# A four-layer sequence model in one launch: layer seams reworked, and the softmax layer's modulation moved from ScalarE to VectorE with one Silu per row of blocks

## The chip, the cores and the metric

The program runs on one core of one Trainium2 chip. The metric is the device time of one execution in microseconds (us), less being better. A change of under 0.2% either way can't be told from no change.

## The reference

The input x is 8 batches of 512 tokens by 512 channels, all float32. It passes four layers in order, each of which adds to x.

```python
# layers 0 and 1 (linear attention), 16 and 8 heads, masks on k and v
xn = layernorm(x); q, k, v = xn @ Wq + bq, xn @ Wk + bk, xn @ Wv + bv
q = softmax(q, over the head's channels); k = softmax(k, over tokens)
y = q @ (k.T @ v)                        # per head
# layer 2 (softmax attention), 16 heads of 32 channels
y = softmax(q @ k.T + mask) @ v
# the end of layers 0 to 2
scale, shift = split(silu(cond) @ W_emb + b_emb)
h = layernorm(y) * (1 + scale) + shift
x = x + silu(h) @ W_out + b_out
# layer 3 (two selective scans, forward and backward)
s = layernorm(x) * (1 + scale) + shift; u = layernorm(s)
z = (u @ Wz + bz) @ Wc + bc; y = scan(z) + z * D      # twice
x = x + gate * ((silu(u @ Wx + bx) * (y1 + y2)) @ Wf + bf + s)
```

## The kernel before

The program is a chain of six blocks, each with its own instruction streams for SP (SyncE, which issues nearly all transfers), TensorE, VectorE (DVE), ScalarE (ACT) and GpSimd (POOL). They run one after the other: `prologue` (folded weights, and the modulation tables `gain` and `shift`), `attention_layer` for layers 0 and 1, `softmax_layer` for layer 2, `front_layer` (norms and input products of layer 3) and `scan_layer`. The place between two blocks is called a seam here. At a seam the block's semaphores are cleared and all engines meet in a barrier (`sems.clear()`, L100). Activations go from layer to layer through HBM tensors `x1`, `x2`, `x3`, one batch (1 MB) at a time. Batch 0 of the next layer is read back, normed and put in `ahead["xn"]` before the seam, and the next K and Q weights are loaded before it too.

**Attention layers.** SP loads the column constants `cols`, the mask row `mask_in`, `rows`, `block_mask` and `keep_in`, then weights 2 and 3, then batch 1. Its last act in a layer is to wait until both `out` buffers are stored (L699). TensorE turns `xn` (stage T, drained by ScalarE with `cols` as scale and bias, L747), then projects K and Q; VectorE drains these, K with `mask_add` and Q with `rows`. Ahead of that VectorE waits for `cols_loaded` and for `const_loaded` (L887, L888), computes `keep`, tells the others that the PSUM banks are free (`absent`, L1018), and computes the mask (L908 or L911). GpSimd meanwhile adds a bias row to all of batch 0 (`residual`, L722).

**Softmax layer.** A batch is 16 steps of four heads and 128 queries. In each step TensorE makes four score tiles (L1303), turns the four tiles of exponentials of the step (L1314) and multiplies the turned tiles of the step before with V (L1330). VectorE takes scores and maxima out of PSUM (L1469) and copies two of the four turned tiles (L1478). ScalarE does four Exp (L1219) and copies the other two (L1228). Work around the attention of batch b is spread over these steps by a list written at build time, `slots`: 28 parts per batch, four each of YT(b-1), T(b+1), K(b+1), TY(b-1), Q(b+1), O(b-1), V(b+1), at most two per step, and all through the one PSUM bank `f_bank`. So each part on TensorE waits until the part before it has been taken out (`filler`, L1256), by the engine that `ENGINE` (L1035) names. TY is the turned, normed y: four transposes, and ScalarE then does Silu with the modulation as scale and bias (L1210). Its four parts stand in steps 7, 7, 8 and 9 of a batch, the first part of Q also in step 9, and the first part of O in step 11. The last batch has YT, TY and O of itself after the last step.

**Front layer.** Per batch TensorE turns `xn`, makes the dlt, B and C columns (L1735, L1743) and mx (L1753, L1700 is its Silu). VectorE does the norms of batch b+1 meanwhile, which end in `xn` (L1820); GpSimd raises the variances to the power of -0.5 (`rsqrt`, L1653) and makes `resid` in three passes over 1 MB (L1663, L1666, L1669). Its order is rsqrt(b), rsqrt2(b), residual(b), and residual(b) starts when `xs` of batch b is there. Batch 0's columns are turned last (`c_turn(B - 1)`), after which C is stored.

**Scan layer.** ScalarE issues loads of `wdt`, `neg_a`, `ident`, `half` and then negates the exponential of `neg_a`; SP loads the first set of `dlt` and `b_tm`, the first `w_z`, then `xn_t`. Every engine waits for all four constants (`const_loaded`). In the steady part GpSimd multiplies states by C (L2034) and VectorE scans (L2350).

The lines with these waits, quoted:

```python
                for j in range(2):
                    sp.wait_ge(x_stored[j], B // 2 * 16 + 16)        # L698, attention layers
    ENGINE = {"YT": "dve", "T": "act", "K": "act", "TY": "act", "Q": "act", "O": "dve", "V": "dve"}   # L1035
                    pool.wait_ge(xs_ready, (b + 1) * TT)             # L1657, residual(b) of the front layer
```

## Time and profile before

| | us |
|---|---|
| median of 3 runs | 5771.74 (5764.97 to 5774.0) |
| profiled execution, its time | 5768.94 |
| its span, first to last instruction | 5766.9 |
| prologue, to about | 200.8 |
| layer 0, to about | 820 |
| layer 1, to about | 1424 |
| layer 2, to about | 2655 |
| front layer, to about | 2992 |
| scan layer, to the end | 5767 |

Busy over the whole span are TensorE 94%, VectorE 73%, ScalarE 52%, GpSimd 50%; the mean granted TensorE clock is 0.984 of full speed. The profile numbers time from the first instruction. In a row of the timeline the last bracket tells how long the engine had been idle before the instruction and which instruction or transfer ended that idle time. A busy share over the span says little here, because the six blocks have different limits; the stretches around the seams and one batch of the softmax layer have to be read each for itself.

### The profile page before, as it was taken

Reading aid. Unit: us, or ns where it says so; the run is one execution under the profiler, and the core shown is the slowest. Engines: PE = TensorE matmul, PEld = TensorE weight load, DVE = VectorE, ACT = ScalarE, POOL = GpSimd, SP = SyncE. Lnnn points to the kernel's source line nnn. Section 1 sums busy time; section 2 is a strip of 40 time slices with the busy share of each in tenths; the row PEclk is TensorE's granted clock in tenths of the full one; section 3 lists DMA queues with packets and bytes.
Section 4 is the critical chain, followed back from the end, with each engine's and each line's share of the span. In section 5 each row is a group of like instructions: output and inputs, shape, how many; then the busy total and the mean of one; then the engine's idle time right before and its main releaser. Section 6 shows DMA issues by size and latency. Waiting matters only on the chain. (4 is left out here: it accounts for less than half of the span.)

```text
span 5766.9 us, 136480 instructions
## 1 busy us (share of the span) xinstructions
PE 5425.2 (94%) x58478; PEld 3270.1 (57%) x58478; DVE 4202.6 (73%) x5872; ACT 2982.9 (52%) x5007; POOL 2907.2 (50%) x956
## 2 busy tenths in 40 slices
PE   8899989998898888987989999999999999999998
PEld 3555545554455555543445566666666666666665
DVE  1455545554455555574429999999999999999996
ACT  0122212222455555551227677777777777776774
POOL 0000000000000000003329999999999999999997
PEclk9999989999999999998999999999999999999999
DMA  6200020111000000003440111212021121111211
GB/s 233 73 33 33 31 70 18 34 34 62 18 1 18 18 18 18 18 19 124 176 152 14 60 57 62 69 54 71 23 62 65 61 70 53 59 35 61 66 59 32
DMA packets 146443, 321.98 MB, mean 56 GB/s; under 512 B 27705, under 2 KB 28474, under 8 KB 135626
## 3 DMA queue, kind: packets, MB, share of 16 engines
q1 hardware_dynamic: 142994, 308.71, 15.8%
q8 instruction: 447, 7.32, 0.5%
q10 hardware_dynamic: 2880, 4.95, 0.2%
q14 instruction: 122, 1.00, 0.1%
HBM read 238.72 MB, written 74.89 MB: 54 GB/s over the span
## 5 line engine op out<-in xcount | busy, mean ns | idle before, releaser
L2034 POOL TENSOR_TENSOR sc_state<-sc_state,sc_c_rows 128x2048 f32<-128x2048 f32 x512 | 2331.3, 4568 | 123.9 <-DVE sc_state L2350 122.7
L2350 DVE TENSOR_TENSOR_SCAN sc_state<-sc_decay,wide 128x512 f32<-128x512 f32 x2048 | 2335.4, 1199 | 27.9 <-PE wide L2208 20.8
L2208 PEld LDWEIGHTS wide<-sc_diag,sc_du_t 64*64 64x64 f32 x32768 | 1047.8, 133 | 526.8 <-issue 344.4
L2208 PE MATMUL wide<-sc_diag,sc_du_t 64*64 64x128 f32 x32768 | 1218.7, 272 | 19.9 <-DVE sc_state L2350 19.7
L2224 PE MATMUL wide<-sc_state,sc_half 64*64 64x512 f32 x8192 | 1199.0, 591 | 7.4 <-POOL sc_state L2034 7.0
L2142 ACT ACTIVATE sc_decay<-sc_delta,sc_neg_a 128x512 f32<-128x512 f32 x1024 | 723.6, 719 | 448.6 <-DVE sc_state L2350 443.5
L2142 ACT ACTIVATE sc_decay<-sc_delta_x,sc_neg_a 128x512 f32<-128x512 f32 x1024 | 710.1, 717 | 286.7 <-DVE sc_state L2350 282.5
L1469 DVE CUSTOM_DVE_ANT_0 l_prob<-wide,l_mask_add 128x512 f32<-128x512 f32 x512 | 339.9, 683 | 275.8 <-PE wide L1303 275.8
L2224 PEld LDWEIGHTS wide<-sc_state,sc_half 64*64 64x64 f32 x8192 | 405.6, 133 | 168.2 <-issue 126.8
L1219 ACT ACTIVATE l_prob<-l_prob,l_s_max 128x512 f32<-128x512 f32 x512 | 366.0, 716 | 231.3 <-DVE l_s_max L1469 231.0
L2181 PE MATMUL wide<-sc_xn_t,sc_w_z 128*128 128x512 f32 x1024 | 476.8, 608 | 1.3 <-DMA sc_xn_t<-xn_d 1.3
L713 POOL TENSOR_SCALAR l_rstd<-l_mv 128x4 f32<-128x4 f32 x16 | 3.8, 236 | 713.9 <-DVE l_mv L902 713.9
L1314 PE MATMUL wide<-ahead_ident,l_prob 128*128 128x128 f32 x2048 | 292.0, 280 | 68.5 <-DVE l_prob_t L1478 41.0
L1314 PEld LDWEIGHTS wide<-ahead_ident,l_prob 128*128 128x128 f32 x2048 | 225.2, 142 | 225.5 <-issue 134.5
L1173 POOL TENSOR_TENSOR l_out<-ahead_x_wk,l_rows 128x2048 f32<-128x2048 f32 x8 | 36.3, 4537 | 603.6 <-DMA x<-l_out 592.0
L2181 PEld LDWEIGHTS wide<-sc_xn_t,sc_w_z 128*128 128x128 f32 x1024 | 185.2, 191 | 210.6 <-issue 210.6
L529 PE MATMUL wide<-l_xn_t,ahead_x_wk 128*128 128x512 f32 x512 | 228.3, 604 | 24.6 <-ACT l_xn_t L747 22.8
L2236 PE MATMUL wide<-sc_w_out,sc_y_sum 128*128 128x256 f32 x1024 | 244.4, 383 | 6.6 <-DVE sc_o_gated L2337 3.6
L747 ACT ACTIVATE l_k_tm<-wide 128x512 f32<-128x512 f32 x64 | 33.1, 606 | 379.4 <-PE wide L520 379.4
L538 PE MATMUL wide<-ahead_w,l_h_t 128*128 128x512 f32 x512 | 226.1, 600 | 1.7 <-ACT l_h_t L747 1.7
L538 PE MATMUL wide<-ahead_w,l_xn_t 128*128 128x512 f32 x512 | 222.5, 592 | 1.0 <-PEq L84 1.0
L538 PE MATMUL wide<-ahead_xn_wq,l_xn_t 128*128 128x512 f32 x512 | 222.5, 592 | 0.6 <-PEq L84 0.6
(240 smaller groups left out, 6983.3 us busy)
## 6 DMA issues: line engine op xcount, KB each, us to landing
sc_c_rows<-c_d SPq DMA_DIRECT2D x64, 1024.0 KB, 4.9
sc_w_z<-wz_tiles SPq DMA_DIRECT2D x128, 256.0 KB, 2.8
x<-l_out SPq DMA_DIRECT2D x24, 1024.0 KB, 4.8
ahead_x_wk<-x SPq DMA_DIRECT2D x16, 1024.0 KB, 6.3
mx_d<-fr_mx SPq DMA_DIRECT2D x16, 1024.0 KB, 4.5
sc_mx<-mx_d SPq DMA_DIRECT2D x64, 256.0 KB, 2.8
pro_wc<-in_wcT SPq DMA_DIRECT2D x4, 2048.0 KB, 19.2
xn_d<-fr_xn_t SPq DMA_DIRECT2D x8, 1024.0 KB, 4.1
```

The source lines that it names most:

```text
L529: last = pe.matmul(bank_of(name, m)[:, :], weight[:, k, m * P:(m + 1) * P], xn_t[:, k, :], start=(k == 0), stop=(k == DT - 1))
L538: last = pe.matmul(bank_of(name, t)[:, :], src_t[:, k, t * P:(t + 1) * P], weight[:, k, :], start=(k == 0), stop=(k == DT - 1))
L1219: act.activation(prob[:, u % (2 * HG), :], prob[:, u % (2 * HG), :], ACT.Exp, scale=-1.0, bias=s_max[:, u % (2 * HG):u % (2 * HG) + 1], ac ...
L1314: last = pe.transpose(t_banks[u % 2][:, m * P:(m + 1) * P], prob[:, u % (2 * HG), m * P:(m + 1) * P], ident[:, :])
L1469: dve.tensor_tensor_reduce(out=prob[:, u % (2 * HG), :], in0=s_banks[i], in1=mask_add[b % 2][:, :], op0=ALU.add, op1=ALU.min, scale=-1.0, ...
L2034: pool.tensor_tensor(state[quad % STATES][:, :, :], state[quad % STATES][:, :, :], c_rows[(r * 4 + q) % ROWS][:, :, :], ALU.mult).then_inc ...
L2142: act.activation(decay[step % DECAYS][:, :], of[:, :], ACT.Exp, scale=neg_a[:, s, m, n:n + 1]).then_inc(decay_ready, 1)
L2181: last = pe.matmul(z_bank, w_z[slot % WZ][:, k, :], xn_t[:, k, :], start=(k == 0), stop=(k == DT - 1))
L2208: last = pe.matmul(to[cols_to, k, :, :], du_t[slot % 2][rows, k, of * 64:(of + 1) * 64], diag[r % 2][rows, c, k, :, :], start=True, stop=True)
L2224: ins = pe.matmul(acc[i][to * 64:(to + 1) * 64, :], half[g * 64:(g + 1) * 64, :], state[quad % STATES][g * 64:(g + 1) * 64, n, :], start=( ...
L2236: last = pe.matmul(z_bank[:, 0:256], y_sum[b % 2][:, k, t * P:(t + 1) * P], w_out[:, k, h * 256:(h + 1) * 256], start=(k == ks[0]), stop=( ...
L2350: dve.tensor_tensor_scan(state[quad % STATES][:, step % 4, order], decay[step % DECAYS][:, order], pair[:, i, order], 0.0, ALU.mult, ALU.a ...
```

## The change

1. **Stores are not waited for at the seams.** `x_stored` and the `out` buffers are now held over layers 0, 1 and 2 by `program`. The wait of SP at the end of a layer is gone. Where a buffer or a batch in HBM is used again, the next layer waits: SP ahead of the load of batch 1, GpSimd ahead of a residual.
2. **Start of an attention layer.** VectorE frees the banks first, then does the mask, then drains K, and only then waits for `const_loaded`, computes `keep` and drains Q. GpSimd's first residual waits for that mask.
3. **Softmax layer.** `ENGINE["TY"]` is "dve": VectorE takes TY out of PSUM with gain and shift (multiply, add). ScalarE does one Silu over all four blocks in place, in SBUF, half a step after the last TY part (behind the first part of Q in its order), and TensorE waits for it ahead of O. For the last batch it stays one Silu per block.
4. **Front layer.** GpSimd's residual(b) also waits for `xn` of batch b. Five small loads go from SP to ScalarE's queue. The last batch's mx is stored in four parts, its C columns are turned and stored earlier, and SP loads the scan layer's first `dlt`, `b_tm`, `xn_t` and `w_z` ahead of the last batch.
5. **Scan layer.** Its constants are loaded in layer 0 and its first set in the front layer, into a tile `set_0` that the prologue and the softmax layer (for `y` and `h_t`) use before. The exponential of `neg_a` comes after the first softplus.

```diff
# attention_layer, SP
-                for j in range(2):
-                    sp.wait_ge(x_stored[j], B // 2 * 16 + 16)
+                for j in range(2):
+                    sp.wait_ge(x_stored[j], stored_ahead)
                 load(1, 1)
# attention_layer, GpSimd
+                pool.wait_ge(mask_ready, 2)
                 residual(0, 0, 0)
# attention_layer, VectorE
-                dve.wait_ge(cols_loaded, 16)
-                dve.wait_ge(const_loaded, 3 * 16)
-                ...
+                first = [i[0] for i in plan].index("T")
+                absent(st, dve, drained["dve"], "dve", -1, plan[0][0], first)
...
+                mask(0, 0, 0)
+                dve.wait_ge(cols_loaded, 16)
+                next_k(-1)
+                dve.wait_ge(const_loaded, 3 * 16)
+                ...
+                next_q(-1)
# softmax_layer
-    ENGINE = {"YT": "dve", "T": "act", "K": "act", "TY": "act", "Q": "act", "O": "dve", "V": "dve"}
+    ENGINE = {"YT": "dve", "T": "act", "K": "act", "TY": "dve", "Q": "act", "O": "dve", "V": "dve"}
+    silu_at = {}
+    for (step, h), parts in slots.items():
+        for name, b, k in parts:
+            if name == "TY" and k == 3:
+                silu_at[step + h, 1 - h] = b
...
-                        ins = act.activation(h_t[:, k, :], f_bank, ACT.Silu, scale=mod_all["gain"][:, layer, k, b:b + 1],
-                                             bias=mod_all["shift"][:, layer, k, b:b + 1])
+                def silu(b):
+                    wait_drained(act, "TY", b, DT - 1)
+                    act.activation(h_t[:, :, :], h_t[:, :, :], ACT.Silu).then_inc(silu_ready, DT)
...
+                        if name == "O" and k == 0:
+                            pe.wait_ge(silu_ready, DT * (b + 1))
...
+                    elif name == "TY":
+                        dve.tensor_scalar(h_t[:, k, :], f_bank, mod_all["gain"][:, layer, k, b:b + 1],
+                                          mod_all["shift"][:, layer, k, b:b + 1], ALU.mult, ALU.add
+                                          ).then_inc(drained["dve"], 1)
# front_layer
                     pool.wait_ge(xs_ready, (b + 1) * TT)
+                    pool.wait_ge(xn_ready, (b + 1) * TT)
...
+                act.dma_start(bf_row[:, :], d["bf_row"].broadcast_to([P, D])).then_inc(const_loaded, 16)
+                act.dma_start(ada[0][:, :, :].rearrange("p r n -> p (r n)"), d["ada_d"][0:1, :].broadcast_to([P, 3 * D])
+                              ).then_inc(ada_loaded[0], 16)
...
-                sp.wait_ge(mx_stored, B * 32)
+                sp.wait_ge(mx_stored, (B - 1) * 32 + 64)
# scan_layer, SP and ScalarE
-                load_set(0)
-                load_w(0)
-                load_xn(0)
-                act.dma_start(wdt[:, :, :, :].rearrange("p s i n -> p (s i n)"), d["wdt"]).then_inc(const_loaded, 16)
...
-                act.wait_ge(const_loaded, 4 * 16)
```

## Rows read from the trace of the kernel before

**Rows 1.** Windows, softmax and scan layer: length, busy PE, PEld, DVE, ACT, POOL, clock.

```profile
1424.00:2655.00 1231.00, 1078.92 (x8576) 601.89 (x8576) 685.82 (x1668) 672.72 (x1466) 57.93 (x43) 0.98 0.05 19
...
2992.00:5767.00 2775.00, 2723.37 (x44032) 1793.77 (x44032) 2681.17 (x2691) 1944.93 (x2939) 2608.14 (x769) 0.99 0.18 57
```

**Rows 2.** Timeline of the seam from layer 0 to layer 1.

```profile
814.83 0.39 SPq L681 DMA_DIRECT2D x<-l_out  x1
...
820.35 0.35 SPq L653 DMA_DIRECT2D l_cols<-in_att_cols  x1
...
827.51 4.70 DVE L911 TENSOR_SCALAR l_mask_add<-l_mask_in 128x512 f32<-128x512 f32 x1
...
828.69 3.34 ACT L747 ACTIVATE l_xn_t<-wide,l_cols 128x512 f32<-128x512 f32 x4 [30.58 <-PE wide L520]
832.08 15.89 PE L529 MATMUL wide<-l_xn_t,ahead_x_wk 128*128 128x512 f32 x32 [0.87 <-ACTq L84]
```

**Rows 3.** Timeline of the seam from prologue to layer 0.

```profile
200.94 0.34 SPq L653 DMA_DIRECT2D l_cols<-in_att_cols  x1
...
213.19 16.43 PE L529 MATMUL wide<-l_xn_t,ahead_x_wk 128*128 128x512 f32 x32 [0.87 <-ACTq L84]
```

**Rows 4.** DMA issues: count, size of each, median us from issue to landing.

```profile
x<-l_out SPq DMA_DIRECT2D x24, 1024.0 KB, 4.8
...
l_mask_in<-in_mask SPq DMA_DIRECT2D x24, 256.0 KB, 7.1
...
l_cols<-in_att_cols SPq DMA_DIRECT2D x3, 16.0 KB, 1.8
```

**Rows 5.** Timeline of ScalarE at the start of layer 2.

```profile
1426.22 0.78 ACT L1204 ACTIVATE l_xn_t<-wide,l_cols 128x512 f32<-128x512 f32 x1 [23.83 <-DMA l_cols<-in_att_cols]
```

**Rows 6.** Timeline of the front layer's start, and its L1820 by source (ns min/median/max).

```profile
2649.85 0.36 SPq L1150 DMA_DIRECT2D x<-l_out  x1
2655.19 1.09 SPq L1602 DMA_DIRECT2D fr_w_dlt<-wdbc_d  x2
...
2695.94 14.44 DVE L1820 TENSOR_SCALAR fr_xn<-fr_xs,fr_mv,fr_rstd 128x512 f32<-128x512 f32 x4 [0.44 <-POOL fr_rstd L1653]
...
2695.88 4.50 POOL L1663 TENSOR_TENSOR fr_resid<-fr_xs,fr_bf_row 128x2048 f32<-128x2048 f32 x1
...
2710.44 3.96 PE L1726 MATMUL wide<-ahead_ident,fr_xn 128*128 128x128 f32 x16 [12.65 <-DVE fr_xn L1820]
...
2752.66 1.04 PE L1726 MATMUL wide<-ahead_ident,ahead_xn_wq 128*128 128x128 f32 x8
...
L1820 DVE TENSOR_SCALAR fr_xn<-fr_xs,fr_mv,fr_rstd x16: 534/542/4720, 2695.9 to 2935.1; 128x512 f32<-128x512 f32 x16
```

**Rows 7.** Timeline of the seam from front to scan layer.

```profile
2986.51 0.36 SPq L1633 DMA_DIRECT2D mx_d<-fr_mx  x1
...
2992.28 0.45 SPq L1898 DMA_DIRECT2D sc_dlt<-dlt_d  x1
...
3002.18 5.96 PE L2181 MATMUL wide<-sc_xn_t,sc_w_z 128*128 128x512 f32 x8 [1.31 <-DMA sc_xn_t<-xn_d]
...
3008.18 0.75 DVE L2301 SCALAR_TENSOR_TENSOR sc_du<-wide,bzc,sc_delta 128x512 f32<-128x512 f32 x1 [4.23 <-PE wide L2181]
```

**Rows 8.** Windows: first TY part to first Q part, softmax batch 2 (columns as rows 1).

```profile
1816.91:1837.47 20.56, 12.22 (x140) 8.18 (x136) 10.26 (x27) 20.35 (x34) 0.00 (x0) 1.00 0.00 1
```

**Rows 9.** Groups by line: ScalarE's table loads; by source: VectorE's PSUM drain with a scalar.

```profile
L1210 ACT ACT_TABLE_LOAD x29 | 37.2, 1283 | 0.5
...
L1769 DVE TENSOR_SCALAR fr_dlt<-wide,fr_dlt_bias x8: 711/750/751, 2694.4 to 2954.3; 128x512 f32<-128x512 f32 x8
```

**Rows 10.** Timeline of TensorE, softmax batch 2: a YT part that VectorE's drain holds.

```profile
1779.09 0.66 PE L1266 MATMUL wide<-ahead_ident,l_y_t 128*128 128x128 f32 x4 [0.49 <-DVE l_y L1444]
```

**Rows 11.** Timeline of ScalarE: the prologue's widest activation; a Q drain of batch 1.

```profile
5.24 1.06 ACT L203 ACTIVATE pro_cond<-pro_cond 8x1024 f32<-8x1024 f32 x1 [0.97 <-DMA ahead_ident<-in_ident]
...
1700.89 0.69 ACT L1208 ACTIVATE l_q_t<-wide,l_cols 128x512 f32<-128x512 f32 x1 [3.43 <-PE wide L1282]
```

More of the change, by code:

```diff
@@ L445, in attention_layer @@
         x = [ahead["x"], sb("x1", [P, TT, D])]
-        out = [sb(f"out{j}", [P, TT, D]) for j in range(2)]
+        out, x_stored = ahead["out"], ahead["x_stored"]
         xn_t = sb("xn_t", [P, DT, T])
@@ L477, in attention_layer @@
         mask_loaded = [sem(f"mask_loaded{j}") for j in range(2)]
-        x_stored = [sem(f"x_stored{j}") for j in range(2)]
+        stored_ahead = layer * B // 2 * 16 + 16
         psum_full = sem("psum_full")
@@ L1069, in softmax_layer @@
         mask_add = [sb(f"mask_add{j}", [P, T]) for j in two]
-        out = [sb(f"out{j}", [P, TT, D]) for j in two]
+        out, x_stored = ahead["out"], ahead["x_stored"]
         xn_t = sb("xn_t", [P, DT, T])
@@ L1128, in _ @@
                 sp.wait_ge(xb_ready, 1)
+                for j in range(2):
+                    sp.wait_ge(x_stored[j], stored_ahead)
                 load(1)
@@ L1538, in _ @@
                 for k in range(4):
+                    drain("TY", B - 1, k)
+                for k in range(4):
                     drain("O", B - 1, k)
@@ L1848, in scan_layer @@
         dp_part = sb("dp_part", [P, 2 * ET])
-        xn_t = sb("xn_t", [P, DT, T])
-        w_z = [sb(f"w_z{i}", [P, DT, P]) for i in range(WZ)]
-        dlt = [sb(f"dlt{i}", [P, T]) for i in two]
-        b_tm = [sb(f"b_tm{i}", [P, 4, N]) for i in two]
+        xn_t, w_z, dlt = first["xn_t"], first["w_z"], first["dlt"]
+        b_tm = [first["b_tm"], sb("b_tm1", [P, 4, N])]
         diag = [sb(f"diag{i}", [P, 8, 4, 64, 2]) for i in two]
@@ L2397, in program @@
         sems = LayerSemaphores(nc)
+        flag = lambda n: ctx.enter_context(nc.semaphore(n))
+        set_0 = sb("set_0", [P, ET, 512])
+        slices = lambda i: set_0[:, i, :].rearrange("p (k n) -> p k n", k=DT)
+        first = {"ident": sb("ident", [P, P]), "half": sb("half", [P, 64]), "wdt": sb("wdt", [P, 2, ET // 2, P]),
+                 "neg_a": sb("neg_a", [P, 2, ET, N]), "b_tm": sb("b_tm0", [P, 4, N]), "xn_t": set_0[:, 0:DT, :],
+                 "dlt": [set_0[:, 4, :], set_0[:, 5, :]], "w_z": [slices(6), slices(7)]}
+        for name in ("const_loaded", "dlt_loaded", "b_loaded", "xn_loaded", "w_z_loaded"):
+            first[name] = flag("first_" + name)
         with ExitStack() as shared:
@@ L2400, in program @@
             pairs = [held("xn_wq", [P, ET, 512]), held("x_wk", [P, ET, 512])]
-            ahead = {"ident": held("ident", [P, P]), "xn": pairs[0][:, 0:TT, :], "x": pairs[1][:, 0:TT, :],
-                     "w": [p[:, TT:ET, :] for p in pairs], "w_mod": pairs}
+            ahead = {"ident": first["ident"], "xn": pairs[0][:, 0:TT, :], "x": pairs[1][:, 0:TT, :],
+                     "w": [p[:, TT:ET, :] for p in pairs], "w_mod": [set_0] + pairs, "scan": first,
+                     "x_stored": [flag(f"x_stored{j}") for j in range(2)]}
             prologue(nc, sems, d, mod_all, banks, ahead)
@@ L2406, in program @@
             ahead["xs"] = held("xs", [P, TT, D])
+            ahead["out"] = [held(f"out{j}", [P, TT, D]) for j in range(2)]
             attention_layer(nc, sems, d, mod_all, banks, 0, d["x"], d["x1"], ahead)
@@ L2414, in program @@
             sems.clear()
-        scan_layer(nc, sems, d, mod_all, wide, out)
+        scan_layer(nc, sems, d, mod_all, wide, out, first)
 def kernel(**inputs):
```

145 lines of the change are left out of this document (78 added, 67 removed).

## The prediction

> **What bounds the kernel now.** I read the windows by block first. The scan layer holds 2775 of 5767 us, with TensorE, VectorE and GpSimd all busy over 93% of it, and the change touches only its start [rows 1]. What the change can move is in the other blocks' seams and in the softmax layer, where TensorE is busy 1078.92 of 1231 us, so about 152 us are idle [rows 1]. For the seams I took the timelines around each block's first instruction, for the softmax layer the windows and the timeline around one batch's TY parts, and for the front layer TensorE's longest wait.
>
> In a seam the reader is to see the last store issued at 814.83 and the next layer's first load only at 820.35, when that store has landed; and then TensorE's K projection as late as 832.08, though its input waits in SBUF [rows 2]. VectorE's mask of 512 columns took 4.70 us, as long as GpSimd's residual beside it, which is why the change puts one behind the other. In the softmax layer, between the first TY part and the first Q part, ScalarE is busy 20.35 of 20.56 us and TensorE 12.22 [rows 8]: ScalarE sets the pace there and only there. In the front layer four small VectorE instructions took 14.44 us, where their line has a median of 0.542 us each, because GpSimd's three residual passes began at 2695.88, and TensorE waited 12.65 us for them [rows 6].
>
> **The change, part by part: the seams.** A wait for a landing is removed. The store lands 4.8 us after its issue [rows 4], so the block starts some 4.4 us earlier (one barrier stays). This is not the whole gain, and not all of it is kept.
>
> Prologue to layer 0: there is no big store, so the start stays. TensorE now turns `xn` at once, ScalarE drains when `cols` lands: 200.94 + 1.8 [rows 3, 4] = 202.8; four drains take 3.34 [rows 2], so K starts at about 206.4 instead of 213.19 [rows 3]: 6.8 us. The mask, 7.1 us after an issue [rows 4], is there before the first K block is full at some 209. TensorE was at half clock here at first; going earlier it meets more of that, so I take 6.3.
>
> Layer 0 to 1: the block starts at about 815.8. But `cols` is queued behind the store of 1 MB. That transfers in SP's queue hold up those behind them, rows 4 show: a mask row of 256 KB, always issued behind a 1 MB load inside the layers, takes 7.1 us, longer than 1 MB alone. So `cols` lands at 814.83 + 4.8 + 0.3 = 819.9, K starts at 819.9 + 3.4 + 0.3 = 823.6 instead of 832.08 [rows 2]: 8.5 us. TensorE's clock stays at half for some of K, which costs another 1 us or so: 7.5. Behind `cols` wait the mask (needed by the first K drain at about 826) and `rows` (needed by Q at 832 or later), and weights 2 and 3 and batch 1 (needed when V starts, near 847), all of which by the time 820.35 to their old use fit. If transfers did not queue, 3 more us would be gained; if `cols` came as late after the store as before, 4 less.
>
> In the Trainium skill, "DMA: Bandwidth & Descriptors", section "Queues, rings and completion order", each DMA engine takes descriptors in ring order. The trace agrees with it (7.1 against 4.8 us). It speaks against the seam part: by it the 4.4 us of the earlier start go mostly to the next layer's first load, and without it the same seam would give 11.
>
> Layer 1 to 2: ScalarE's first drain at 1426.22 waits for `cols` [rows 5]; by the same queueing it lands at about 1424.3. 1.7 us (0 to 4.4).
>
> Layer 2 to front: store 2649.85, first load 2655.19 [rows 6]. TensorE's transposes start 4.4 us earlier, but ScalarE first issues five loads (two such issues took SP 1.09 us) and `w_dlt` queues behind the store, so batch 0 gains 3. Then the residual. With GpSimd's passes behind `xn`, VectorE's four instructions take 4 x 0.54 less overlap = 1.9, and `xn` of batch 1 is ready before TensorE ends batch 0, whose end comes at about 2695 (2710.44 - 12.65 - 3). Batch 1 starts there instead of at 2710.44: 15.4. TensorE then does not come out of an idle stretch: batch 1 took 42.2 us (2710.44 to 2752.66), the six later ones 38.97 each ((2986.51 - 2752.66)/6) [rows 6, 7]; 3 of these 3.2 us go. Together 18. What waits behind the moved residual: rstd of the next batch stands behind it in GpSimd's order, and VectorE's norm of the next batch waits for that. Residual(b) now starts when `xn`(b) is done, 10 us ahead of TensorE's batch b, and takes 13.7 (3 passes); the norm chain after it takes some 11; that ends about 16 us into a batch of 39, and VectorE is held there anyway until the C columns are turned, some 25 us in. So it is hidden, with 10 us to spare. If the cover were gone, each of six batches would lose what it lacks.
>
> Front to scan: the last mx store (2986.51 [rows 7]) is 512 KB instead of 1 MB with a C store behind it: 2.4 us. The first z product no longer waits for `xn_t`. Before, `du` came at 3008.18, 15.9 us after the layer's start at 2992.28 [rows 7]. After, dt products take some 2 us and the z product its 5.96, so `du` comes 8.3 us after the start: 7.6. ScalarE's table load and softplus (5 us) are hidden behind these. Together 10 (8 to 13; the upper end is a z product at full clock).
>
> Seams and front: 6.3 + 7.5 + 1.7 + 18 + 10 = 43.5.
>
> **The softmax layer.** Removed from ScalarE per batch: four Silu out of PSUM (0.78 each) and eight table loads, Silu and back, of 1.283 [rows 9]: 13.4 us of its 20.35 [rows 8]. Added: one Silu of 2048 columns and two table loads. No such activation is in the trace. From 0.69 us for 512 columns and 1.06 for 1024 [rows 11], 0.37 per 512 more, it is 1.8; its bounds are 1.06 and four times 0.78. So a burst of 1.8 + 2.6 = 4.4 us. It stands behind the first Q drain, where a Q part keeps TensorE for at least the 3.43 us that ScalarE idled before a Q drain [rows 11]. Between the end of Q part 1 and TensorE's first need of an exponential that ScalarE has not made yet lie scores, two turned tiles, values, Q part 2, two more tiles and Q part 3: two times 3.43 and some 4 us of attention work, 11 us, against 0.7 for the drain, 4.4 for the burst and 1.4 for two Exp. Cost 0; if that cover is not there, 4.4 per batch.
>
> Added to VectorE: four drains per batch out of PSUM, 0.75 each at most [rows 9], 3 us. In the stretch its busy time goes from 10.26 to 13.3, more than TensorE's 12.22 [rows 8], so VectorE is next in line. The stretch can't get shorter than 13.3, and at worst stays at 20.56. The nearest pattern is YT, transposes that VectorE drains: there TensorE is held by 0.49 us for the part after [rows 10]. TensorE's own 12.22 and four such holds are 14.2; with VectorE 94% full beside it I take 14.6, a saving of 6 in each of batches 1 to 6. Batch 7 has no Q part to hide the burst behind; there I take 5. Together 6 x 6 + 5 = 41. The tail gets four VectorE drains and then one more Silu before O, about 0.4 us more, and nothing to gain; that is within the rounding. Softmax: 41, bounds 0 and 7 x 7.3 = 51.
>
> The Trainium skill, "ScalarE: Activation LUTs", section "What ACT_TABLE_LOAD costs", gives a switch 1283 ns and a drain of about 1380 ns besides. The row agrees on the load alone; no row here shows a drain behind it. By it the 42 removed switches would be 112 us of ScalarE instead of 54, but the saving would still be bounded by what TensorE needs.
>
> Sum: 43.5 + 41 = 84.5. The profiled execution took 5768.9, so 5684.4; the median of the runs is 2.8 above it: **5687**.
>
> **The rivals.**
> *A, VectorE takes ScalarE's place.* For: 13.3 of busy time in order with its other waits. Against: the hold behind a YT part is only 0.49 [rows 10]. If each of the 28 TY parts holds TensorE by 0.7 us more than that, half the softmax gain goes, 84.5 - 20 = 64.5: 5707.
> *B, the seams give back more.* For: five more loads, `wx` and batch 1's loads share the engines with the store, and TensorE's clock stays low longer after short bursts. If three seams lose 4 us each and the front 5: 5704.
> *C, more.* If loads do not queue behind the store (+3 and +3) and TensorE keeps its full clock in the seams (4 to 6), 5675.
> *D, the change does not do what it says:* the moved residual comes onto the chain. Its 10 us of slack would have to be wrong; 13.7 us for six batches are 82, and the sum is about 0: 5770.
> *E, slower.* The steady scan slows. `xn_t`, `w_z` and `dlt` now share one tile at another address and all later tiles move. VectorE scans and GpSimd's multiplications fill 2681 and 2608 of 2775 us [rows 1], so any per-instruction growth is on the chain. From 3.1% (85 of 2775) it undoes all else; at 4% the time is 5687 + 111 = 5798. Against: nothing in the rows ties a scan's time to its address.
>
> **How the numbers follow.** All parts within a few us of their sizes: 0.62, own range 5678 to 5697. A 0.13, B 0.10, C 0.10, D 0.03, E 0.02. What differs by less than 0.2% (11.5 us) can't be told from no change. Faster: the first four, 0.95; same: D, 0.03; slower: E, 0.02. The range takes in A, B and C with some of their spread: 5668 to 5713.
>
> **What would show it.** Right: K starts 7 to 11 us after each attention layer's first instruction; L1820 never above 0.6 us and no wait of over 2 us of TensorE for it; 16 table loads in the softmax layer instead of 58; 14 to 15 us from the first TY part to the first Q part, with VectorE the fullest; `du` some 8 us after the scan's start; the rest of the scan layer as long as before. Wrong: `cols` landing later than 5.5 us after the store, TensorE waiting on VectorE's L1478 more than before, waits for rstd in the front layer, or longer scans.

## The result and the profile after

The changed kernel takes 5681.72 us (median of 4 runs, 5680.99 to 5688.06), where the kernel before, run beside it, took 5771.05: a ratio of 0.9849, 95% interval 0.9832 to 0.9866. The forecast was 5687 us, range 5668 to 5713. The profiled execution has a span of 5679.5 us instead of 5766.9, 87.4 less, against a forecast sum of 84.5.

I cut both traces at the same events: the first load of layer 0, the last store of each attention layer, the first TY part, TensorE's last batch of the front layer, the first `du`, the end.

| stretch | before, us | after, us | shorter by | forecast |
|---|---|---|---|---|
| prologue, to layer 0's first load | 200.94 | 199.05 | 1.9 | 0 |
| to layer 0's last store | 613.89 | 602.16 | 11.7 | 6.3 |
| to layer 1's last store | 604.22 | 595.18 | 9.0 | 7.5 |
| to the softmax layer's first TY part | 249.11 | 248.04 | 1.1 | 1.7 |
| to its last store | 981.69 | 941.84 | 39.9 | 41 |
| to the front layer's batch 7 | 296.93 | 282.94 | 14.0 | 18 |
| to the first `du` of the scan layer | 61.40 | 51.82 | 9.6 | 10 |
| to the end | 2758.7 | 2758.5 | 0.2 | 0 |

Layer 0 of this execution was a short one: with the same code for it, `seams_only` (below) shows 603.92 us. At the end of this layer the granted clock stood at 0.50 for 6.8 us here (from 779.1) and for 10.2 us there (from 779.8); in the prologue, whose code did not change, for 3.4 us here and 6.8 in the kernel before. So some 2 us of the 11.7, and the 1.9 in the prologue, come and go with TensorE's clock.

The seam from layer 0 to 1, timeline of the changed kernel (it answers to rows 2):

```profile
801.21 0.39 SPq L691 DMA_DIRECT2D x<-ahead_out  x1
802.80 0.35 SPq L654 DMA_DIRECT2D l_cols<-in_att_cols  x1
...
803.73 3.65 PE L520 MATMUL wide<-ident,ahead_xn_wq 128*128 128x128 f32 x16 [3.40 <-DVEq L84]
...
806.71 2.78 ACT L756 ACTIVATE l_xn_t<-wide,l_cols 128x512 f32<-128x512 f32 x4 [20.43 <-DMA l_cols<-in_att_cols]
...
808.50 0.43 DVE L915 TENSOR_SCALAR l_mask_add<-l_mask_in 128x512 f32<-128x512 f32 x1 [7.43 <-DMA l_mask_in<-in_mask]
809.55 1.22 PE L529 MATMUL wide<-l_xn_t,ahead_x_wk 128*128 128x512 f32 x1 [2.17 <-ACTq L84]
```

The first load is issued 1.6 us after the store and not 5.5. TensorE turns `xn` at once; ScalarE's first drain is what waits for `cols`, 5.5 us after the store. The mask takes 0.43 us instead of 4.70, with GpSimd now waiting for it. K starts 8.3 us after the store, where it was 17.3 [rows 2].

In the softmax layer, windows as in rows 1 and 8: the whole layer, the stretch from the first TY part to the first Q part of batch 2, and the scan layer:

```profile
1396.39:2586.27 1189.88, 1075.78 (x8576) 600.23 (x8576) 713.51 (x1700) 610.29 (x1403) 57.83 (x43) 0.98 0.06 20
...
1785.11:1799.34 14.23, 11.93 (x141) 8.21 (x137) 13.15 (x31) 9.76 (x26) 0.00 (x0) 1.00 0.01 2
...
2913.30:5679.50 2766.20, 2722.57 (x44032) 1793.27 (x44032) 2681.96 (x2691) 1944.70 (x2939) 2608.05 (x769) 1.00 0.17 56
```

The stretch of 20.56 us [rows 8] is 14.23 us, with VectorE busy for 13.15 of it (forecast 14.6 and 13.3), ScalarE for 9.76 instead of 20.35. Groups of the softmax layer, ScalarE's new instructions, VectorE's new drain and TensorE's waits in its turned tiles:

```profile
L1225 ACT ACTIVATE set<-set 128x2048 f32<-128x2048 f32 x7 | 13.4, 1912 | 0.1
L1232 ACT ACT_TABLE_LOAD x8 | 10.3, 1283 | 0.1
L1225 ACT ACT_TABLE_LOAD x7 | 9.0, 1283 | 0.1
...
L1473 DVE TENSOR_SCALAR set<-wide,gain,shift 128x512 f32<-128x512 f32 x32 | 25.8, 806 | 10.7 <-PE wide L1294 10.6
...
L1334 PE MATMUL wide<-ident,l_prob 128*128 128x128 f32 x2048 | 291.7, 279 | 51.9 <-DVE l_prob_t L1500 48.7 <-ACT l_prob_t L1241 2.0
```

With the tail's one there are 16 table loads, as forecast. The Silu takes 1.91 us (estimate 1.8), the drain 0.81 (0.75). TensorE's wait for ScalarE's `l_prob_t` is 2.0 us over the layer, and the same group of the kernel before has 26.4:

```profile
L1314 PE MATMUL wide<-ahead_ident,l_prob 128*128 128x128 f32 x2048 | 292.0, 280 | 68.5 <-DVE l_prob_t L1478 41.0 <-ACT l_prob_t L1228 26.4 <-ACT l_prob L1219 0.4
```

The wait for VectorE's `l_prob_t` rose from 41.0 to 48.7 us, which the prediction had named as a sign of being wrong. It is not the moved drain: run 3 below, where VectorE has no TY drain, shows 48.3. One of the bursts, ScalarE's timeline after a Q drain:

```profile
1803.08 0.69 ACT L1220 ACTIVATE l_q_t<-wide,l_cols 128x512 f32<-128x512 f32 x1 [2.69 <-PE wide L1300]
1803.78 1.28 ACT L1225 ACT_TABLE_LOAD   x1
1805.08 1.91 ACT L1225 ACTIVATE set<-set 128x2048 f32<-128x2048 f32 x1
1807.01 1.28 ACT L1232 ACT_TABLE_LOAD   x1
1808.30 0.72 ACT L1232 ACTIVATE l_prob<-l_prob,l_s_max 128x512 f32<-128x512 f32 x1
```

It is 4.5 us from the first load to the next exponential, with no gap. The Trainium skill, "ScalarE: Activation LUTs", section "What ACT_TABLE_LOAD costs", adds a drain of about 1380 ns to each switch; this timeline shows 1.28 us a switch and nothing behind it. By the same section's formula for an activation with immediate scale and bias an estimate is 186 + 0.833 x 2048 = 1892 ns; the row says 1912.

The front layer (it answers to rows 6):

```profile
2586.27 0.36 SPq L1165 DMA_DIRECT2D x<-ahead_out  x1
...
2587.70 0.46 ACTq L1716 DMA_DIRECT2D fr_bf_row<-in_bf_row  x1
...
2588.44 1.97 PE L1769 MATMUL wide<-ident,ahead_xn_wq 128*128 128x128 f32 x8 [2.99 <-DVEq L1828]
...
2592.24 1.45 ACT L1736 ACTIVATE fr_xn_t<-wide,ssm_cols 128x512 f32<-128x512 f32 x2 [26.77 <-issue]
...
2598.28 5.42 PE L1778 MATMUL wide<-fr_xn_t,fr_w_dlt 128*128 128x512 f32 x8 [3.25 <-DMA fr_w_bc<-wdbc_d]
2598.30 4.50 POOL L1697 TENSOR_TENSOR fr_resid<-ahead_xs,fr_bf_row 128x2048 f32<-128x2048 f32 x1 [10.50 <-DMA fr_dlt_bias<-dbc_bias_d]
...
2607.06 27.69 PE L1796 MATMUL wide<-fr_xn_t,fr_wx 128*128 128x512 f32 x64
...
2634.58 1.04 PE L1769 MATMUL wide<-ident,fr_xn 128*128 128x128 f32 x8
...
2660.35 1.90 DVE L1864 TENSOR_SCALAR ahead_xn_wq<-ahead_xs,fr_mv,fr_rstd 128x512 f32<-128x512 f32 x4
...
2673.41 1.04 PE L1769 MATMUL wide<-ident,ahead_xn_wq 128*128 128x128 f32 x8
```

Batch 1 starts 48.3 us after the store (60.6 before) without a wait, batch 2 another 38.8 later (42.2 before). `xn` of batch 2 is ready at 2662.3, 11 us before TensorE wants it: the slack was forecast at 10. VectorE idles 12.5 us for rstd in each of batches 2 to 7, and this costs TensorE nothing. No instruction of L1864 lasts over 0.55 us. But batch 0's large products start 20.8 us after the store, no sooner than before (20.3): ScalarE's first drain stands behind its own five issues, and the dt product then waits for `w_bc`.

The scan layer's start (it answers to rows 7):

```profile
2913.49 1.97 PE L2195 MATMUL wide<-set,wdt 64*64 64x512 f32 x4 [4.85 <-PEq L100]
...
2915.38 5.61 PE L2213 MATMUL wide<-set 128*128 128x512 f32 x8
...
2921.03 0.75 DVE L2332 SCALAR_TENSOR_TENSOR sc_du<-wide,bzc,sc_delta 128x512 f32<-128x512 f32 x1 [2.55 <-PE wide L2213]
```

`du` comes 7.7 us after the layer's start at 2913.30 (15.9 before, 8.3 forecast).

### The profile page after: what moved, and what is told of

Its sections match the earlier page's. It is cut to its first block and busy times, and to the rows that moved or that the text cites. A ratio compares the mean times of both kernels' runs of the same rounds, so it can differ in the third digit from the quotient of the medians.

```text
span 5679.5 us, 136465 instructions
## 1 busy us (share of the span) xinstructions
PE 5410.8 (95%) x58478; PEld 3262.1 (57%) x58478; DVE 4209.2 (74%) x5904; ACT 2919.1 (51%) x4944; POOL 2906.6 (51%) x956
## 5 line engine op out<-in xcount | busy, mean ns | idle before, releaser
L2070 POOL TENSOR_TENSOR sc_state<-sc_state,sc_c_rows 128x2048 f32<-128x2048 f32 x512 | 2330.2, 4564 | 122.8 <-DVE sc_state L2381 121.4
L2381 DVE TENSOR_TENSOR_SCAN sc_state<-sc_decay,wide 128x512 f32<-128x512 f32 x2048 | 2335.2, 1198 | 28.0 <-PE wide L2240 20.8
L2256 PE MATMUL wide<-sc_state,half 64*64 64x512 f32 x8192 | 1199.5, 592 | 7.5 <-POOL sc_state L2070 7.0
L2174 ACT ACTIVATE sc_decay<-sc_delta,neg_a 128x512 f32<-128x512 f32 x1024 | 723.6, 719 | 448.7 <-DVE sc_state L2381 443.6
L2174 ACT ACTIVATE sc_decay<-sc_delta_x,neg_a 128x512 f32<-128x512 f32 x1024 | 710.1, 717 | 286.7 <-DVE sc_state L2381 282.5
L2256 PEld LDWEIGHTS wide<-sc_state,half 64*64 64x64 f32 x8192 | 405.8, 133 | 168.6 <-issue 127.5
L2213 PE MATMUL wide<-set 128*128 128x512 f32 x1024 | 476.2, 608 | 0.0
L1334 PEld LDWEIGHTS wide<-ident,l_prob 128*128 128x128 f32 x2048 | 224.8, 142 | 209.6 <-issue 136.3
L1334 PE MATMUL wide<-ident,l_prob 128*128 128x128 f32 x2048 | 291.7, 279 | 51.9 <-DVE l_prob_t L1500 48.7
L1185 POOL TENSOR_TENSOR ahead_out<-ahead_x_wk,l_rows 128x2048 f32<-128x2048 f32 x8 | 36.3, 4532 | 563.5 <-DMA x<-ahead_out 549.9
L2213 PEld LDWEIGHTS wide<-set 128*128 128x128 f32 x1024 | 185.1, 191 | 208.7 <-issue 208.7
```

What stands on the lines that cost most here:

```text
L1334: last = pe.transpose(t_banks[u % 2][:, m * P:(m + 1) * P], prob[:, u % (2 * HG), m * P:(m + 1) * P], ident[:, :])
L2070: pool.tensor_tensor(state[quad % STATES][:, :, :], state[quad % STATES][:, :, :], c_rows[(r * 4 + q) % ROWS][:, :, :], ALU.mult).then_inc ...
L2174: act.activation(decay[step % DECAYS][:, :], of[:, :], ACT.Exp, scale=neg_a[:, s, m, n:n + 1]).then_inc(decay_ready, 1)
L2213: last = pe.matmul(z_bank, w_z[slot % WZ][:, k, :], xn_t[:, k, :], start=(k == 0), stop=(k == DT - 1))
L2256: ins = pe.matmul(acc[i][to * 64:(to + 1) * 64, :], half[g * 64:(g + 1) * 64, :], state[quad % STATES][g * 64:(g + 1) * 64, n, :], start=( ...
L2381: dve.tensor_tensor_scan(state[quad % STATES][:, step % 4, order], decay[step % DECAYS][:, order], pair[:, i, order], 0.0, ALU.mult, ALU.a ...
```

## The experiments

Times are medians of 4 runs (5 for the last). The kernel before ran beside them each time: its medians were 5774.47 us beside runs 1 to 4, 5771.28 beside runs 5 to 8 and 5769.75 beside runs 9 to 12. The 95% intervals of the ratios are some 10 us wide to either side, so differences of a few us between two of these kernels are read from the traces.

**1 and 2. Each half alone.** `soft_only` is the kernel before with the softmax layer's edits:

```
-ENGINE = {... "TY": "act", ...}
+ENGINE = {... "TY": "dve", ...}
+    act.activation(h_t[:, :, :], h_t[:, :, :], ACT.Silu).then_inc(silu_ready, DT)
```

> The kernel before with the softmax layer's change alone. My theory: the softmax part is worth 36 us in the six middle batches and 5 in the last, and nothing of the seams' gain hangs on it, so this kernel takes 5771 - 40 = 5731 us (5726 to 5736), and the stretch from the first TY part to the first Q part lasts some 14.3 us. Rival, the parts are not additive (the softmax change saves more when the seams are old, or part of the seams' gain is really the softmax layer's): below 5722 or above 5740.

5727.12 us, ratio 0.9918 (0.9902 to 0.9935): 47 us faster than the kernel before. Its softmax layer, store to store, lasts 1187.64 us against 1230.80: 43.2. Its first five batch periods (from the first TY part of one batch to that of the next) are all near 140.6 us; in the changed kernel two of these five are 142.3, each with a stretch of 3.4 us at a granted clock of 0.50.

`seams_only` is the changed kernel with those edits undone.

> The changed kernel with the softmax layer's drains and Silus as they were before (Silu out of PSUM on ScalarE, four per batch). My theory: the seams and the front layer are worth the rest, 87.4 - 39.8 = 47.6 us of the profiled executions, so 5771 - 48 = 5723 us (5718 to 5728), with 20.5 us from the first TY part to the first Q part. Rival, the parts are not additive: below 5713 or above 5733.

5726.29 us, ratio 0.9917 (0.9900 to 0.9933): 48 us faster. Its softmax layer lasts 1231.42 us, as before. The halves add up: by the medians 47 + 48 = 95 against 89 for both together, which the intervals allow, and by the spans of the profiled executions 44.6 + 41.8 = 86.4 (5722.3 and 5725.1 against 5766.9) against 87.4. Nothing of the gain needs both.

**3 and 4. Which edit of the softmax layer pays.** `act_drain_one_silu` keeps the drain on ScalarE, without the table switch:

```
-    dve.tensor_scalar(h_t[:, k, :], f_bank, gain, shift, ALU.mult, ALU.add)
+    act.activation(h_t[:, k, :], f_bank, ACT.Identity, scale=gain, bias=shift)
```

> The changed kernel, but ScalarE takes the modulation out of PSUM itself (Identity with scale and bias, four per batch) and then does the one Silu; VectorE has no TY drain. Theory one, table loads and the burst's place were what mattered: ScalarE has 9.8 + 4 x 0.78 = 12.9 us of work in a stretch of 14.2 us, VectorE 9.9, and TensorE's 12 still set it: the stretch stays at 14 to 15 us and the time within 4 us of the changed kernel (5678 to 5686). Theory two, the move to VectorE was what mattered, since ScalarE's drains stand in line behind its exponentials: each of 28 TY parts holds TensorE by at least 0.5 us more, 5696 or above.

5675.62 us (5668.97 to 5675.95), ratio 0.9828 (0.9812 to 0.9845). It is 6 us *faster* than the changed kernel, 2.4 below theory one's range. The two ratios' intervals overlap; the traces decide: its softmax layer lasts 1173.33 us, and 1177.20 in run 12, which has the same drains, where the eight traces with VectorE's drain and one Silu, the changed kernel's 1189.88 among them, lie between 1187.6 and 1191.5. (The last batch too gets one Silu over all four blocks here: from its first TY part to the store it takes 32.0 us instead of 29.5.) `dve_drain_four_silus` keeps VectorE's drain and brings back a Silu, and its table loads, for each part:

```
-    act.activation(h_t[:, :, :], h_t[:, :, :], ACT.Silu).then_inc(silu_ready, DT)
+    act.activation(h_t[:, k, :], h_t[:, k, :], ACT.Silu).then_inc(silu_ready, 1)
```

> The changed kernel with VectorE's TY drains, but ScalarE does a Silu of 512 columns for each part, half a step after its drain, instead of one for all four: 8 table loads per batch instead of 2. Theory one, table loads matter: ScalarE gets 6 x 1.283 + (4 x 0.63 - 1.91) = 8.3 us more work per batch, 9.8 + 4 x 0.63 + 8 x 1.283 = 22.6 us in a stretch of 14.2 us, so exponentials come late and TensorE waits for them: the stretch goes to 20 us or more and the time to 5681.7 + 6 x 6 = 5718 us or above. Theory two, only TensorE's wait for the drain mattered, and ScalarE's lateness is absorbed by the slack behind: within 5 us of the changed kernel.

5710.20 us, ratio 0.9886 (0.9869 to 0.9902). Both theories missed the size: the stretch is 18.3 us, not 20, nor unchanged. With the two, all four combinations of drain and Silu have been run; the shortest batch period in batches 1 to 4:

| us per batch | four Silus | one Silu |
|---|---|---|
| ScalarE drains | 146.9 (before) | 138.9 |
| VectorE drains | 144.5 | 140.7 (after) |

One Silu is worth 8.0 us a batch with ScalarE's drains and 3.8 with VectorE's. Moving the drain is worth 2.4 us while ScalarE is clogged with table loads, and *costs* 1.7 once it isn't. The 144.5 holds a stretch of 3.4 us at half clock, as every batch of that run does (the clock of 0.91 below); the other three cells have none. By an estimate from these 3.4 us it would be 1.7 us less without it; the 3.8 would then be 2.1 and the 2.4 be 4.1, and the signs stay. No run separates having fewer table loads from having them later: one Silu does both, as the burst now stands behind the stretch. Windows of the stretch, `act_drain_one_silu` first, then `dve_drain_four_silus`:

```profile
1784.58:1797.11 12.53, 11.45 (x140) 8.20 (x137) 10.08 (x26) 11.22 (x27) 0.00 (x0) 1.00 0.01 2
```

```profile
1791.82:1810.10 18.28, 13.55 (x141) 9.34 (x137) 13.42 (x31) 16.97 (x31) 0.00 (x0) 0.91 0.00 1
```

With ScalarE's drains TensorE has 11.45 us of work in 12.53, no engine fuller. (The first Q part starts at 1797.21, so the stretch itself is 12.63 us.) Where VectorE's drain costs is in TensorE's timeline: the second TY part starts 1.79 us after the first with ScalarE's drain (1784.58, 1786.37) and 2.56 us with VectorE's. The changed kernel:

```profile
1786.81 0.81 DVE L1473 TENSOR_SCALAR set<-wide,gain,shift 128x512 f32<-128x512 f32 x1
...
1787.67 0.66 PE L1294 MATMUL wide<-ident,set 128*128 128x128 f32 x4 [0.61 <-DVE set L1473]
...
1799.34 1.12 PE L1300 MATMUL wide<-l_xn_t,ahead_xn_wq 128*128 128x512 f32 x2 [0.61 <-DVE set L1473]
```

The first tile was full at 1785.8; VectorE, which works in order, was in a copy and did a row maximum first. Two such holds a batch, 0.77 us each, are 1.5 of the 1.7.

**5. The residual behind `xn`.** `resid_before_xn` is the changed kernel without one line:

```
 pool.wait_ge(xs_ready, (b + 1) * TT)
-pool.wait_ge(xn_ready, (b + 1) * TT)
```

> The changed kernel without GpSimd's wait for xn ahead of the front layer's residual, so that its three passes begin beside VectorE's norm instructions again. My theory: batch 1 starts some 12 us later and its TensorE work meets half clock for another 3 us: 5681.7 + 16 = 5698 us (5694 to 5702), L1864 of batch 1 again at some 4 us each. Rival, with the seams changed this wait is hidden or was caused by the late start: within 4 us of the changed kernel.

5690.64 us (5689.41 to 5695.91). TensorE and VectorE in the front layer:

```profile
2595.04 0.36 SPq L1165 DMA_DIRECT2D x<-ahead_out  x1
...
2632.72 14.48 DVE L1863 TENSOR_SCALAR fr_xn<-fr_xs,fr_mv,fr_rstd 128x512 f32<-128x512 f32 x4 [0.44 <-POOL fr_rstd L1686]
...
2647.25 3.67 PE L1768 MATMUL wide<-ident,fr_xn 128*128 128x128 f32 x16 [2.66 <-DVE fr_xn L1863]
```

The collision is back in full (14.48 us for four instructions), yet batch 1 starts 52.2 us after the store and batch 2 91.9, only 3.9 and 4.7 later than in the changed kernel, not 12 and 16. Against the kernel before (60.6 and 102.8) 8.4 and 10.9 us are there without the wait. They come from the loads: GpSimd's first residual starts 11.8 us after the store here and 12.0 in the changed kernel, 20.2 in the kernel before, where its row was SyncE's last load but batch 1's. Batch 1's rstd stands behind that residual, and `xn` behind rstd.

That does not make the loads two thirds of the gain, for the two edits cover each other. In the trace of `act_drain_one_silu`, whose front layer is the changed kernel's, the first of ScalarE's five issues took 4.4 us instead of 0.5, and the first residual started as late as 19.0 us after the store (issued at 2573.28):

```profile
2592.28 4.53 POOL L1695 TENSOR_TENSOR fr_resid<-ahead_xs,fr_bf_row 128x2048 f32<-128x2048 f32 x1 [17.47 <-DMA fr_dlt_bias<-dbc_bias_d]
...
2618.21 1.92 DVE L1862 TENSOR_SCALAR fr_xn<-fr_xs,fr_mv,fr_rstd 128x512 f32<-128x512 f32 x4 [0.44 <-POOL fr_rstd L1684]
...
2621.63 1.04 PE L1767 MATMUL wide<-ident,fr_xn 128*128 128x128 f32 x8
```

Batch 1 still starts 48.3 us after the store and batch 2 87.2, as in the changed kernel. With the wait in place 7 us of delay to the residual cost nothing; with the collision's 12.6 us more (14.48 - 1.92) batch 1 would have started at about 59 (an estimate from these rows). So the wait is worth 3.9 us behind an early residual and by that estimate some 11 behind a late one, and the earlier loads are worth 8.4 us without the wait and, by this trace, nothing with it.

Of the 8.9 us that the runs show, the trace explains 5.3 (up to `du`); the rest is in layers whose code is the same.

**6. The landing of the stores.** `stores_awaited` puts the waits back:

```
+for j in range(2):
+    sp.wait_ge(x_stored[j], stored_ahead + B // 2 * 16)
```

> The changed kernel with SyncE's waits for the last stores' landing back at the end of the three attention layers. Theory one, loads queue behind the store anyway, so most of the 4 us of earlier start was given back: the first drain needs cols, which would land 1.8 us after an issue that comes 5.5 us after the store, at 7.3 us instead of 5.5 in the seam from layer 0 to 1 and instead of 4.9 in the next, and the front layer loses 2 to 3: together 6 us, 5688 (5685 to 5691). Theory two, no queueing matters and each seam loses the whole 4 us: 5694 or above. Theory three, the landing is hidden altogether: within 2 us of the changed kernel.

5688.13 us, 6.4 more than the changed kernel, as theory one had it; the traces, read below by layer, show 5.7. The same seam:

```profile
807.98 0.39 SPq L691 DMA_DIRECT2D x<-ahead_out  x1
813.36 0.35 SPq L654 DMA_DIRECT2D l_cols<-in_att_cols  x1
...
815.42 3.34 ACT L758 ACTIVATE l_xn_t<-wide,l_cols 128x512 f32<-128x512 f32 x4 [24.19 <-PE wide L520]
...
818.81 13.56 PE L529 MATMUL wide<-l_xn_t,ahead_x_wk 128*128 128x512 f32 x27 [0.87 <-ACTq L84]
```

Issued 3.8 us later, `cols` lands in at most 2.1 us instead of 3.9, and K starts 10.8 us after the store instead of 8.3. By layer the wait costs 2.4 us (to layer 1's first output), 1.0 and 2.3: so of 3.8 us of earlier start each seam keeps 1 to 2.5.

**7. Whose queue.** `cols_own_queue` lets ScalarE issue the load of `cols`:

```
-sp.dma_start(cols[:, :], d["att_cols"][:, layer, :])
+act.dma_start(cols[:, :], d["att_cols"][:, layer, :])
```

> The changed kernel, but ScalarE issues the load of cols, the first that each attention layer needs, on its own queue instead of SyncE's. Theory one, that load lands late because it stands behind the 1 MB store in SyncE's queue: on another queue it lands about 1.8 us after its issue instead of 3.9 and 3.3, and layers 1 and 2 start their first drains some 2 and 1.5 us earlier: 5678 us. Theory two, it is late because the 16 DMA engines are busy with the store whatever the queue: it lands as late as before and the time stays at 5681.7. Both are within the spread of the timed runs; the timeline decides.

5686.08 us (5683.46 to 5690.86), no gain. The timeline decides:

```profile
808.09 0.39 SPq L690 DMA_DIRECT2D x<-ahead_out  x1
...
809.69 0.37 ACTq L750 DMA_DIRECT2D l_cols<-in_att_cols  x1
...
813.94 2.78 ACT L756 ACTIVATE l_xn_t<-wide,l_cols 128x512 f32<-128x512 f32 x4 [22.59 <-DMA l_cols<-in_att_cols]
```

4.25 us after its issue, against 3.91 from SyncE's queue (in the next seam 3.69 against 3.28). The load is late while a store of 1 MB is under way, whichever engine issued it. My "queued behind the store in SP's queue" is refuted as the mechanism. The Trainium skill, "DMA: Bandwidth & Descriptors", section "Queues, rings and completion order", has each DMA engine take turns between queues packet by packet; by that alone another queue should have helped, and here it did not. The same section lets the write that reports a landing go through only after every earlier write of that DMA engine, across its queues. The traces agree with that: in the two seams `cols` landed 0.4 and 0.2 us after the store in the changed kernel, and 1.4 and 0.2 us after it from ScalarE's queue. No run shows whether its data were there sooner.

**8 and 9. The front layer's first loads.** `front_weights_first` gives ScalarE the two loads of `w_dlt`, moves its five others behind batch 0's drains, and lets TensorE wait for `w_dlt` and `w_bc` apart:

```
-act.dma_start(bf_row...); act.dma_start(ada[0]...); act.dma_start(bc_bias...); ...
+act.dma_start(w_dlt[:, :, s, :], fused[:, s, :, 0:R]).then_inc(w_dlt_loaded, 16)
-pe.wait_ge(w_dbc_loaded, 64)
+pe.wait_ge(w_dlt_loaded, 32)
```

> The changed kernel, but at the front layer's start ScalarE issues only the two loads of w_dlt (not the five of biases and rows, which it issues after batch 0's drains), and TensorE waits for w_dlt and w_bc apart. My theory: batch 0 of this layer gave back the 3 us that I had forecast for it, because ScalarE's first drain stood 3.8 us behind its five issues and the dt product waited for w_bc: now the dt product starts about 6 to 9 us after the store instead of 12, and the batch ends 3 to 5 us earlier: 5678 us. Rival, wx (2 MB) lands too late anyway, and batch 0's large products wait for it: no change.

5682.18 us: no change.

```profile
2588.24 0.36 SPq L1165 DMA_DIRECT2D x<-ahead_out  x1
...
2603.09 27.73 PE L1800 MATMUL wide<-fr_xn_t,fr_wx 128*128 128x512 f32 x64 [0.34 <-DMA fr_wx<-in_wxT]
...
2606.87 4.54 POOL L1695 TENSOR_TENSOR fr_resid<-ahead_xs,fr_bf_row 128x2048 f32<-128x2048 f32 x1 [17.10 <-DMA fr_dlt_bias<-dbc_bias_d]
...
2634.77 3.62 PE L1771 MATMUL wide<-ident,fr_xn 128*128 128x128 f32 x16 [3.95 <-DVE fr_xn L1868]
```

The large products start 14.8 us after the store, 5.9 sooner. But the residual starts at 18.6 instead of 12.0, batch 1's `xn` is late behind it, TensorE waits 3.95 us for it and comes out at half clock: batch 2 starts 86.2 us after the store against 87.1. `front_two_queues` has SyncE load the residual's rows ahead of batch 1's:

```
+sp.dma_start(bf_row...).then_inc(bf_loaded, 16); sp.dma_start(ada[0]...)
 load(1)
```

> As front_weights_first, but SyncE issues the row and the ada rows that GpSimd's first residual needs ahead of batch 1's loads, with a semaphore of their own, and ScalarE only the small biases behind its drains. Theory one, front_weights_first won 6 us up to batch 0's large products and lost them again because the residual began 8 us later and batch 1's rstd stands behind it in GpSimd's order: now GpSimd starts by some 12 us after the store, batch 1 starts some 43 us after the store instead of 48.3, and the time falls by about 5 us to 5677. Theory two, what came late was batch 1's own loads and norm, not the residual: batch 1 starts at 46.5 us after the store or later, 5680 to 5682.

5682.74 us. Batch 1 starts 44.9 us after the store and batch 2 83.7, 3.4 and 3.5 sooner, `du` only 2.0 sooner; the residual still starts 17.0 us after the store, and TensorE waits 1.08 us for `xn`. Direction as in theory one, size less than half; the timed runs can't tell 2 us.

**10. `cols` kept in SBUF.**

```
-cols = sb("cols", [P, 8 * DT])
+cols = mod_all["att_cols"][:, layer, :]
```

> The changed kernel with the att_cols of all three attention layers kept in SBUF from the prologue on (384 bytes more per partition), so that no layer loads cols at its start. Theory one, after the change cols is what the seams end on: ScalarE's first drain comes as soon as TensorE has turned a tile, K of layer 1 starts some 6 us after the store instead of 8.3, the first drain of layer 2 some 2.5 us after it instead of 4.9, K of layer 0 gains 1: together 5 to 6 us, 5676. Theory two, the next load takes its place (the mask, rows or a weight lands too late and K's drains or TensorE wait for it), or TensorE's half clock takes most of it back: 5680 to 5682.

5680.09 us (5677.27 to 5681.51). In the seam from layer 0 to 1:

```profile
806.61 0.39 SPq L690 DMA_DIRECT2D x<-ahead_out  x1
...
809.81 2.78 ACT L754 ACTIVATE l_xn_t<-wide,att_cols 128x512 f32<-128x512 f32 x4 [19.91 <-PE wide L520]
...
812.64 11.85 PE L529 MATMUL wide<-l_xn_t,ahead_x_wk 128*128 128x512 f32 x27 [1.57 <-ACTq L84]
```

K starts 6.0 us after the store and layer 1's first output is 4.1 us nearer to it; in layer 2 it is 2.2. Layer 0's K does not come sooner (4.8 us). TensorE never falls to half clock in that seam: from 808.0 to 816.6 it is granted 1.00, where the changed kernel has 0.51 and 0.53 up to 813.5. The trace shows the 6 us that theory one wants; the time shows 1.6, within the spread.

**11. Two drains on each engine.** `split_drains`:

```
+return "act" if name == "TY" and k % 2 else ENGINE[name]
```

> The changed kernel with parts 0 and 2 of TY drained by VectorE and parts 1 and 3 by ScalarE (Identity), and the one Silu behind them. The period of a softmax batch is 140.67 us with four drains on VectorE and 138.95 with four on ScalarE. Theory one, each VectorE drain behind which TensorE has a part to turn costs its own hold of 0.6 us or so (parts 0 and 3 here showed a wait): a period of 139.5 to 140, 5677 us. Theory two, what counts is that no engine is nearly full in the stretch (VectorE at 13.15 of 14.23 us): with 11.6 on VectorE and 11 on ScalarE the period is 138.5 or less, 5672 us or below.

5677.39 us, period 139.8. That is half way between four and none on VectorE, and only one of the two holds is left (the second TY part starts 2.56 us after the first, the first Q part 1.78 after the last TY part): each drain's own hold counts, as in theory one, not how full an engine is.

**12. The better kernel.** `combined` is `act_drain_one_silu` with `cols` resident and the loads of `front_two_queues`.

> The changed kernel with three edits of the runs before: ScalarE drains TY (Identity) and then does the one Silu, cols of all layers stay in SBUF, and the front layer's loads are those of front_two_queues. If the gains add up: 6 to 12 us from the softmax layer, 5 from cols, 5 from the front layer, so 5681.7 - 19 = 5663 us (5656 to 5668). If only the softmax layer's part holds: 5672 to 5676.

5663.15 us (5661.65 to 5667.94, 5 runs), ratio 0.9814 (0.9801 to 0.9828), whose interval lies below the changed kernel's. 18.6 us less than the changed kernel, where the forecast was 19. Span against span (5662.5 and 5679.5) it is 17.0: softmax layer 12.7 by its stores, layer 1 5.8, front to `du` 3.8, less 4.8 in prologue and layer 0 (where the changed kernel's execution was the short one) and 0.5 in the scan layer.

## Why the prediction held, and where it did not

*The sum* was right (84.5 against 87.4), and 5687 is 5 us from the median. Part of that is luck: the terms missed by +1.9 (prologue), +5.4, +1.5, -0.6, -1.1, -4.0, -0.4 and +0.2, and some 4 us of the first two are TensorE's clock in parts that the change leaves alone.

*Prologue to layer 0, 6.3.* K starts 4.75 us after the first load instead of 12.25: 7.5, forecast 6.8. I had TensorE meet more of its half clock; it met less. In the kernel before the first 4 us of K ran at a granted clock of 0.50, in the changed one at 1.00: it had idled 3.3 us ahead of the transposes instead of 10.6. K's 32 products took 14.0 us instead of 16.4. 7.5 and 2.4 are the 9.9 us by which `seams_only` is shorter; the other 1.8 of the 11.7 are this execution's clock at the layer's end.

*Layer 0 to 1, 7.5, and 1 to 2, 1.7.* 8.9 by K's start and 9.0 by the stores; 2.3 by the first drain, 1.1 by the first TY part. `cols` landed 5.5 and 4.9 us after the store, forecast 5.1. The number was right and its mechanism wrong: the step that failed is "that transfers in SP's queue hold up those behind them". Run 7 shows the delay is no matter of the queue, run 6 that it goes away once the store has landed. The number held because the load lands just behind the store either way.

*Layer 2 to front, 18.* 15.7 by batch 2, 14.0 by batch 7. The step that failed is "batch 0 gains 3": it lost 0.5, behind five issues on ScalarE and `w_bc`; I had named the five issues and priced them too low, and missed that the dt product waits for all four weight loads. So batch 1 starts 48.3 us after the store and not 45.2, though, as forecast, when TensorE ends batch 0 and not when `xn` comes. The collision of GpSimd's passes with VectorE is real (run 5), and with a late residual the wait for `xn` takes all of it away (the trace of run 3). What I did not see is that five loads on ScalarE's queue also let the first residual start 8 us sooner, which alone brings batch 1 8.4 us forward. The 1.7 us between batch 2 and batch 7 are a stretch of 3.4 us at half clock (from 2755.4). The slack behind the moved residual, 10 us, was 11.

*Front to scan, 10.* 9.6, step by step as told.

*Softmax, 41.* 39.9. The six middle batches gave 35.6 (36 forecast), batch 7 5.0 (5), the tail took 0.7 (0.4). The stretch gained 6.3 in each; the six periods gained 4.1 to 8.1, since stretches of 3.4 us at half clock, worth 1.7 each, fell in other batches than before. The burst is hidden, as argued. What I did not see is that the drain's move was no part of the gain. Rival A, VectorE in ScalarE's place, was real in kind: 1.7 us a batch against ScalarE's own drains, where I had priced it at 2.8 (four holds of 0.7). Two holds of four came, and the 14.6 us, which had room for four, was 14.23. Its cure is not to move the drain at all (run 3).

*Rivals.* C's first half has some truth: with `cols` out of the way the seams give 6 us more by the trace. B did not come. D and E are refuted: slack of 11 us, and 2758.5 us from `du` to the end against 2758.7, with VectorE's scans at 1198 ns each (1199 before) and GpSimd's multiplications at 4564 (4568).

*Signs.* Most came as told, three did not. K starts 4.8, 6.8 and 10.1 us after the first load of layers 0, 1 and 2, not 7 to 11; the range did not fit the prediction's own 5.5 and 7.8 for the first two. TensorE's wait for VectorE's turned tiles rose by 7.7 us and VectorE waits for rstd in the front layer, both named as signs of being wrong; the first is there without the moved drain too, and the second ends before TensorE wants the result.

## What to carry to other kernels

An engine that looks overloaded with a function may be overloaded with table loads: take those away first, by one instruction per row, and measure again before moving its drains to a neighbour that works in order. Where two edits act on one wait, run each alone: here moving the drain was worth +2.4 us with four Silus and -1.7 with one. And what an edit is worth can hang on which other is in place: in the front layer the moved loads gave 8.4 us without the wait for `xn` and nothing with it, so taking one edit out does not give its share of the gain.

## What the runs showed of the hardware

A load of 16 KB issued 1.6 us behind a store of 1 MB takes 3.9 us on the store's queue and 4.25 on another; issued when the store has landed, at most 2.1. The store itself lands 4.2 us after its issue with nothing behind it, and 5.0 in the seam from layer 0 to 1 with loads issued from 1.6 us on. Four VectorE instructions of 512 columns beside GpSimd's passes over 128x2048 took 14.5 us in both kernels where they collide, 1.9 where they don't; a mask of 512 columns 4.70 and 0.43. In the seam from prologue to layer 0 TensorE, after 3.3 us without work, made its 16 transposes at a mean granted clock of 0.66 and K at 1.00; after 10.6 us it made both at 0.50, K for the first 4 us. In the seam from layer 0 to 1 of the changed kernel, with two stretches of 3.4 and 2.2 us without work, it went on at 0.53 for 4 us; in `cols_resident`, with 3.4 and 1.6, at 1.00.
